# A token tower on one core: orders of five engines and homes of the banks by a plan of eleven steps with 27 added waits, in place of one of thirteen with 37

## The reference, cut to what matters

```python
h = take(table, x)                                   # embedding, f32
h = h + linear_attention(layernorm(h))               # L0_attn: elu features, cumulative sums in each row of 128 tokens
h = h + (layernorm(h) @ CB.T) * scale + bias         # L0_ffn
h = h + performer_block(layernorm(h))                # L1_attn: softmax features, projection, ff 256->1024->256, two norms
x = layernorm(h)                                     # L1_ffn
logits = x @ router_w.T                              # 8 experts, one is chosen for each token
xs = x * sigmoid(max(logits))
moe = (silu(xs @ gate[e]) * (xs @ up[e])) @ down[e]  # e = argmax(logits)
h = h + moe + silu(x @ shared_gate) * (x @ shared_up) @ shared_down
```

## Time and profile before

| | us |
|---|---|
| median of 3 runs | 658.73 (656.73 to 664.01) |
| the profiled execution | 657.52 |
| its span in the trace | 655.7 |
| PE busy | 617.5 |
| DVE busy | 466.2 |
| ACT busy | 317.8 |
| POOL busy | 278.4 |

### The profile page before, as it was taken

One profiled execution on the slowest core, in us unless ns is written; L12 is line 12 of the kernel. 1 busy time (PEld: TensorE's weight loads), 2 busy tenths in 40 slices (PEclk: granted clock), 3 DMA queues, 4 the chain that ended last, 5 costly groups with the idle time before them and its releaser, 6 DMA issues.

```text
span 655.7 us, 15603 instructions
## 1 busy us (share of the span) xinstructions
PE 617.5 (94%) x5960; PEld 503.3 (77%) x5960; DVE 466.2 (71%) x1108; ACT 317.8 (48%) x751; POOL 278.4 (42%) x534
## 2 busy tenths in 40 slices
PE   5987899999999999999999999999999698999997
PEld 4765688988888989898989889999999554554563
DVE  3697998999999988888889989768657432223322
ACT  3456576667566654756555556565332021212321
POOL 6263357345464353534333263352332334535433
PEclk9899999999999999999999999999999999999999
DMA  7960000000000000000000000000001259363551
GB/s 257 411 286 1 9 10 9 2 10 17 2 20 9 9 18 2 17 2 19 1 18 17 2 18 2 17 19 10 17 25 34 58 215 401 113 227 115 193 215 32
DMA packets 17369, 46.88 MB, mean 71 GB/s; under 512 B 6913, under 2 KB 11536, under 8 KB 14864
## 3 DMA queue, kind: packets, MB, share of 16 engines
q1 hardware_dynamic: 13136, 37.47, 15.2%
q0 software_dynamic: 4160, 8.41, 4.0%
HBM read 40.54 MB, written 6.89 MB: 72 GB/s over the span
## 4 chain that ended last, share of the span: by engine, by line
PE 77%; DVE 7%; DMA 6%; issue 3%; ACT 3%; POOL 2%; SPq 2%; POOLq 0%; DVEq 0%; ACTq 0%
PE ps L1150 71%; PE ps L1155 3%; DMA we<-w_experts 2%; PE ps L1311 2%; DMA home_rows<-send_home 1%; DMA x_rows<-send_x 1%; DVE stats L751 1%; SPq L318 1%; SPq L319 1%; DMA H_S<-table,idx_sb 1%; POOL rstd L422 1%; ACT qkA L729 1%; DVE rdenTA L826 1%; DVE H_S L803 0%; PE ps L1285 0%
## 5 line engine op out<-in xcount | busy, mean ns | idle before, releaser
L421 POOL TENSOR_TENSOR var_eps<-mv,ln_eps 128x1 f32<-128x1 f32 x112 | 24.2, 216 | 252.7 <-DVE mv L752 251.7
L1150 PE MATMUL ps<-yTC,we 128*128 128x128 f32 x1024 | 124.3, 275 | 0.0
L1150 PEld LDWEIGHTS ps<-yTC,we 128*128 128x128 f32 x1024 | 120.5, 192 | 1.0 <-issue 0.3
L1150 PE MATMUL ps<-we,yTA 128*128 128x256 f32 (+1 forms) x272 | 86.7, 449 | 4.3 <-issue 3.7
L422 POOL TENSOR_TENSOR rstd<-var_eps,pow_half 128x1 f32<-128x1 f32 x112 | 66.2, 591 | 8.8
L1150 PEld LDWEIGHTS ps<-we,yTA 128*128 128x128 f32 x272 | 49.7, 191 | 25.2 <-issue 21.1
L1150 PE MATMUL ps<-we,ffT 128*128 128x256 f32 x256 | 60.8, 380 | 0.0
L1150 PE MATMUL ps<-we,yTB 128*128 128x256 f32 (+1 forms) x176 | 52.9, 442 | 2.1 <-SPq L367 2.1
L1150 PEld LDWEIGHTS ps<-we,ffT 128*128 128x128 f32 x256 | 47.2, 190 | 5.6
L1150 PEld LDWEIGHTS ps<-we,yTB 128*128 128x128 f32 x176 | 32.0, 190 | 16.8 <-issue 13.9
L803 DVE TENSOR_TENSOR H_S<-ps,causal_sb 128x512 f32<-128x512 f32 x64 | 40.0, 668 | 2.2 <-PE ps L1150 2.2
(11 more groups left out here) (220 smaller groups left out, 1341.5 us busy)
## 6 DMA issues: line engine op xcount, KB each, us to landing
we<-w_experts SPq DMA_DIRECT2D x8, 1536.0 KB, 17.1
H_S<-w_experts SPq DMA_DIRECT2D x8, 1536.0 KB, 6.6
we<-w_ff SPq DMA_DIRECT2D x2, 1024.0 KB, 8.7
x_rows<-send_x SPq DMA_DIRECT2D x16, 128.0 KB, 1.7
home_rows<-send_home SPq DMA_DIRECT2D x16, 128.0 KB
rows_sb<-rows SPq DMA_DIRECT2D x1, 1664.0 KB
we<-w_qk SPq DMA_DIRECT2D x2, 512.0 KB
we<-w_v SPq DMA_DIRECT2D x2, 256.0 KB
```

The source lines that it names most:

```text
L421: link(pool.tensor_tensor(var_eps[:, k:k + 1], mv[:, k, 1:2], ln_eps[:], ALU.add))
L1150: return pe.matmul(o, a, b, start=start, stop=stop)
```

## The change

The steps, their operations, operands and numbers are the same. What changes is the order of each engine's list, the lags, the bank of each result, and the added waits (27). PE's lags reach 11, hence 27 turns; DVE's 11, ACT's 10, POOL's 10, SP's 8. The waits for operands stay. The banks of the experts' part are numbered afresh too.

```diff
-        dgT, T0, qk0, v0, nd0, o0 = (ps[:, 5, :], ps[:, 6, :], ps[:, 2, :], ps[:, 4, :], ps[:, 5, :], ps[:, 7, :])
+        dgT, T0, qk0, v0, nd0, o0 = (ps[:, 7, :], ps[:, 6, :], ps[:, 6, :], ps[:, 2, :], ps[:, 3, :], ps[:, 0, :])
...
             run_steps([
-                (4, home_out), (0, x_out), (9, ids2), (3, ids1), (9, ids3), (1, ids0),
+                (3, home_out), (1, ids0), (6, ids1), (8, ids2), (0, x_out), (8, ids3),
             ])
...
             def a_T0(t):
                 pe.wait_ge(S["src0_ready"], t + 1)
-                after(pe, "qexp_in", (t - 5) * 2 + 2)
-                after(pe, "scores_masked", (t - 2) * 4 + 1)
                 transposed(T0, yA).then_inc(S["src0T_psum"], 1)
...
             def a_v(t):
                 pe.wait_ge(S["src0T_ready"], t + 1)
-                after(pe, "ffb_ready", (t - 6) * 4 + 4)
-                after(pe, "v0_ready", t)
+                after(pe, "scores_masked", (t - 1) * 4 + 1)
...
             def b_kq(t):
...
                 if t + 3 < T:
                     after(pe, "scores_masked", (t + 3) * 4 + 3)
-                if t + 4 < T:
-                    after(pe, "x_ready", (t + 4) * 4 + 4)
+                after(pe, "tile_done", t - 6)
...
             def c_dn(t):
                 pe.wait_ge(S["hT_ready"], t + 1)
-                if t + 6 < T:
-                    after(pe, "out1_read", t + 7)
-                if t + 3 < T:
-                    after(pe, "logit_copied", t + 4)
+                if t + 9 < T:
+                    after(pe, "src1T_ready", t + 10)
...
             run_steps([
-                (6, b_out), (1, a_v), (11, c_ga), (0, a_T0), (5, b_kmB), (4, a_ffn), (7, c_f1), (12, c_dn),
...
+                (7, c_f1), (5, b_v), (5, b_kmB), (1, a_v), (4, a_ffn), (11, c_up), (9, c_cn), (7, c_f2), (8, c_T6),
+                (3, a_out), (10, c_ga), (8, c_lo), (6, c_T5), (2, a_num), (5, b_ctx), (2, a_den), (4, b_T3),
+                (5, b_qT), (5, b_cTT), (0, a_T0), (4, b_qk), (1, a_s), (11, c_dn), (0, a_qk), (5, b_h), (4, b_dg),
+                (4, b_kq), (4, b_dgT), (6, c_fa), (6, c_fb), (3, a_T2), (5, b_out), (4, b_kmT),
             ])
```

More of the change, by code:

```diff
@@ L709, in _ @@
             run_steps([
[L710 to L713, removed]
+                (10, c_th), (0, a_norm), (2, a_rd), (5, b_cT), (8, c_tt), (4, b_yT), (5, b_rqT), (1, a_par),
+                (0, a_yT), (5, b_cx2), (3, a_norm2), (4, b_x), (4, b_sq), (0, a_x), (8, c_send), (4, b_dgc),
+                (7, c_norm), (4, b_rk), (6, c_ra), (3, a_yT2), (0, a_exp), (6, c_rb), (4, b_ek), (4, b_keps),
+                (7, c_yT2), (4, b_eq), (3, b_norm), (5, c_yT),
             ])
@@ L1117, in _ @@
             run_steps([
[L1118 to L1122, removed]
+                (0, a_stats), (6, b_rec), (5, b_dgr), (6, b_mean), (5, b_km), (5, b_qs), (5, kmx), (6, b_o),
+                (5, b_ks), (6, b_x1), (4, a_ff), (5, b_vo), (9, c_slot), (1, a_max), (10, table2), (11, c_hid),
+                (9, table0), (7, c_o), (10, table3), (3, a_o), (8, c_log), (7, c_res), (1, a_elu), (10, c_gc),
+                (9, table1), (1, a_vz), (3, a_res), (2, a_rec), (5, b_cx), (2, a_mean), (1, a_m1), (1, a_m2),
+                (1, a_m3), (11, c_down), (8, c_choose), (1, a_m0),
             ])
@@ L1227, in a_out @@
                 pe.wait_ge(S["src1T_ready"], t + 1)
+                if t + 1 < T:
+                    after(pe, "scores_masked", (t + 1) * 4 + 3)
                 by_token(o0[:, 0:D], yTA1, out0_sb, KD).then_inc(S["out0_psum"], 1)
@@ L1238, in a_ffn @@
                 pe.wait_ge(S["src2T_ready"], t + 1)
+                if t + 2 < T:
+                    after(pe, "scores_masked", (t + 2) * 4 + 2)
                 by_token(ff0[:, 0:D], yTA2, cb_sb, KD).then_inc(S["ffn0_psum"], 1)
@@ L1242, in b_T3 @@
                 pe.wait_ge(S["src3_ready"], t + 1)
+                after(pe, "src5T_ready", t - 1)
                 transposed(T3, yB).then_inc(S["src3T_psum"], 1)
@@ L1358, in c_fa, with c_fb @@
                 pe.wait_ge(S["src5T_ready"], t + 1)
+                after(pe, "ff2_read", t)
+                by_channel(fa, yTC, ff1_sb, range(4)).then_inc(S["ffa_psum"], 1)
+            def c_fb(t):
+                if t == 0:
+                    pe.wait_ge(S["last_loaded"], 16 * 7)
+                pe.wait_ge(S["src5T_ready"], t + 1)
                 if t + 5 < T:
                     after(pe, "scores_masked", (t + 5) * 4 + 4)
-                by_channel(fa, yTC, ff1_sb, range(4)).then_inc(S["ffa_psum"], 1)
-            def c_fb(t):
-                pe.wait_ge(S["src5T_ready"], t + 1)
-                if t + 2 < T:
-                    after(pe, "diag_read", t + 3)
-                after(pe, "hT_ready", t - 4)
+                after(pe, "gC_ready", t - 3)
                 by_channel(fb, yTC, ff1_sb, range(4, 8)).then_inc(S["ffb_psum"], 1)
@@ L1432, in _ @@
             run_steps([
-                (6, b_out), (1, a_v), (11, c_ga), (0, a_T0), (5, b_kmB), (4, a_ffn), (7, c_f1), (12, c_dn),
-                (3, a_out), (9, c_cn), (5, b_qT), (7, c_f2), (2, a_num), (5, b_ctx), (2, a_den), (4, b_T3), (8, c_T6),
-                (6, c_T5), (5, b_cTT), (4, b_qk), (1, a_s), (0, a_qk), (11, c_up), (5, b_h), (4, b_dg), (4, b_kq),
-                (8, c_lo), (4, b_dgT), (6, c_fa), (3, a_T2), (6, c_fb), (4, b_kmT), (4, b_v),
+                (7, c_f1), (5, b_v), (5, b_kmB), (1, a_v), (4, a_ffn), (11, c_up), (9, c_cn), (7, c_f2), (8, c_T6),
+                (3, a_out), (10, c_ga), (8, c_lo), (6, c_T5), (2, a_num), (5, b_ctx), (2, a_den), (4, b_T3),
+                (5, b_qT), (5, b_cTT), (0, a_T0), (4, b_qk), (1, a_s), (11, c_dn), (0, a_qk), (5, b_h), (4, b_dg),
+                (4, b_kq), (4, b_dgT), (6, c_fa), (6, c_fb), (3, a_T2), (5, b_out), (4, b_kmT),
             ])
```

63 lines of the change are left out of this document (25 added, 38 removed).

## The result

660.93 us median (659.53 to 665.36, 20 runs) against 658.16 (654.28 to 664.71, 20 runs) of the kernel before: a ratio of 1.006, with a 95% interval of 1.0043 to 1.0077 (the two medians alone give 1.004). That is 0.6% slower, clear of no change but less than 1%. The profiled execution took 660.82 us, its span 659.0 us.

A forecast was written before the change was run, and what follows sets the result against it. PE's own work was taken as the bound in the middle. The terms 2.0 + 1.8 + 1.5 - 2.4 + 2.7 summed to +5.6 us, a span of 661.3 and an execution of 663.1 us, with a range of 655 to 670.

The forecast's parts named there:

- Added waits and banks, 0: Whole pipeline: ten fewer added waits and new banks change nothing, as met waits cost nothing visible; ends -1.5 and +1.5.
- no order can win more than those 3.1 us there: Middle of the kernel: PE's own work bounds it, with some 1.7 us lost per 100 us at most.
- The fill, +2.0: Start of the pipeline: `a_v` and `a_T0` behind `b_kmB` cost +2.6 over tiles 0 and 1, less 0.6 at `b_kq`.
- The two waits: Fill, as a sign: PE idle about 2 us right before `km_diag`'s matmul, twice, before 85 us.
- One more `c_up`, +1.8: Drain: one more `c_up` stands ahead of the last `c_cn` on PE and moves all behind it by 1.8 us.
- `c_down` ahead of `c_choose`, +1.5: Drain, DVE: the last `c_choose` stands behind `c_down`, which waits for a `home_rows` store slowed by a scatter; +1.5 us.
- SP's order, -2.4: Drain and late experts: one store less in the way, late weights load some 4 us sooner, ending waits; -2.4 us.
- The clock, +2.7: Start of the experts' part: PE mostly idles before the rows come, so its clock falls to 0.50; +2.7 us.
- the slower case: Each turn: ACT's steps between `a_den` and `a_s` stall PE, 0.5 us in 13 turns, +6.5; 668 to 672; chance 0.16.
- the faster rival: Fill and drain: a shorter pipeline pays, two tiles' waits (-4) and 3.2 us of drain idle go; -9, about 650; chance 0.10.

The follow-up runs named there:

- ten_waits: The changed kernel with ten more added waits on PE at `a_s`, all long met; 662.62 us, ratio 1.0088 to the kernel before.
- before_yt: The kernel before with one ACT step moved, `c_yT` ahead of `a_par`, `b_cx2` and `a_rd`; 654.79 us, ratio 0.9967 to the kernel before.
- place_up: The changed kernel with `c_down` adding into H (no store wait) and `c_up` behind `c_cn` on PE; 660.34 us, ratio 1.0045 to the kernel before.
- in_place: The changed kernel with `c_down` adding into the tile's rows of H, so without the store wait; 661.25 us, ratio 1.0058 to the kernel before.
- sp_old: The changed kernel with SP's list of the kernel before; 662.67 us, ratio 1.0073 to the kernel before.
- warm_gap: The changed kernel with 56 small matmuls behind PE's last pipeline step and 24 behind the experts' first transposes; 664.89 us, ratio 1.0088 to the kernel before.
- kmb_early: The kernel before with PE's `b_kmB` ahead of `a_v`, `c_ga` and `a_T0`; 667.40 us, ratio 1.0172 to the kernel before.

## Why the prediction was right, and where it was not

The time, 663 against 660.9, and the verdict (within 1%, on the slower side) were right, but partly by luck: errors in the sum have opposite signs. Between the two traces, in us of the span:

| part | predicted | measured |
|---|---|---|
| fill, up to `b_qk` of tile 2 | +2.0 | +3.3 |
| middle, from there to the last `c_f2` | 0 | -2.4 |
| the last `c_cn` (one more `c_up`, `c_down`) | +3.3 | +2.0 |
| from `c_cn` to the first product | 0 | +0.7 |
| first round (clock) | +2.7 | +2.2 |
| late weights | -2.4 | -2.2 |
| together (measured: with a rest of -0.3) | +5.6 | +3.3 |

- *Added waits and banks, 0.* That met waits cost nothing was right (`ten_waits`). The step that failed is the reading of the middle, "no order can win more than those 3.1 us there". It took busy time for work. A `b_qk` that takes 2.04 us is as busy as one of 1.95, and the turn fell by 0.46 us with PE busy as before. Of this 0.21 are ACT's late `c_yT`, shown by `before_yt`; 0.25 lie between or within other steps and are not settled. From `b_qk` of tile 7 to that of tile 12, five turns, it is 150.29 us before and 147.90 in the changed kernel, so 2.4 us came from the full turns. The two new idle times of the middle cost 0.37 + 1.17 us once; without them the middle would have won some 4 us (2.4 + 1.5), which is above the 3.1.
- *The fill, +2.0.* Measured +3.3. The two waits came as described. But in these traces their own cost is about 0.2 us; 3.1 are a fall of the clock that the prediction did not expect there: PE was busy 6.27 of the 10 us from 50 to 60, as before 6.21. The kernel before and `before_yt` have one order there, one without the fall and one with it, so the fall is not the order's alone. The 0.97 ahead of `b_kq` went, and `b_kq` started only 0.06 sooner.
- *One more `c_up`, +1.8.* It is there as work, but moving it back wins nothing (`place_up`): `c_choose` was not done sooner, and PE would have waited in its place. As a loss by the order it was not real.
- *`c_down` ahead of `c_choose`, +1.5.* The mechanism was right: the store took 8.24 us, and PE waited 2.17. `in_place` removes the wait in the trace; that the time falls with it no run shows. The route to the rows was seen less well: `c_slot` is behind `c_down` too.
- *SP's order, -2.4.* The wait went, and PE's last `c_dn` ended 14.2 us after `c_cn`, as said, with the loads at 26.8. But the list was not needed for it (`sp_old`).
- *The clock, +2.7.* Right: 5.90 us for 3.69, +2.2, at the place forecast, and in `warm_gap`, with the idle time filled, it is 3.69 again. All ten traces in which PE waited 1.1 us or more for the first rows, with nothing put into that time, have a slow first round (5.2 to 6.7 us); `before` and `before_yt`, without such a wait, do not. One trace speaks for a second cause: in `kmb_early` PE waited 0.25 us only, and the round took 5.09. The gain of `warm_gap` did not reach the time, though.

Of the rivals, no stall came between `a_den` and `a_s`, which was the slower case.

Two figures of the prediction do not follow from its rows, and the sum does not hang on either: PE's work behind the last `c_cn` is 14.77 us by the window and not 15.3, and the two terms of the faster rival, 4 and 3.2 us, make 7.2 and not 9.

The clock is more of the result than the profile of one execution tells. The mean granted clock of the 20 runs of the changed kernel was 0.981, that of 89 runs of the kernel before 0.987 (the profiled ones had 0.983 and 0.994). Among the 20, the twelve at 0.982 and above took 659.53 to 661.76 us, the eight below 662.35 to 665.36. Read as a slope, which is 0.47 us for each 0.001 both in these 20 and in the 89, 0.006 is some 3 us: about the whole difference between the two medians. That does not clear the orders, because the clock is no cause apart from them: one fall of 6.8 us takes 0.005 off the mean of 659 us. As an estimate, the changed kernel has about one such fall more than the kernel before has on average. It also means that the profiled execution of the kernel before flatters it: of the 89 only five had 0.994 or more.

No version here beats both kernels for certain. `before_yt` has the lowest median, 654.79 us, and its interval ends at 1.0001.

## What to carry to other kernels

Busy time is not work: where an engine is busy 99% of the time, take the pitch of one full turn, and of each step in it, before saying that no order can win. Many met waits are cheap, and one that is met late in every turn is not. A fall of TensorE's clock for 6.8 us cost 2 to 3 us here, more than a wait of 2 us ahead of it; it comes in some executions of the same instructions and not in others, so compare several traces before giving it to an order. Where a wait vanishes, look what it hid. A mean clock for each run belongs beside each time.

## What the hardware showed unexpectedly

- The clock fell at 56.0 us in the changed kernel, with no idle time of PE over 1.98 us in the 6 us ahead. In `before_yt` it fell at 55.2 behind the same instructions, and the same 7.06 of 10 us busy, at which it stayed up in the kernel before. Filled, it fell 24 us later, for 3.4 us and not 6.8.
- Ten waits for semaphores long met, on one step, left a full turn at 29.61 us.
- A store of 128 KB took 8.24 us beside a scatter of 128 numbers of 4 bytes, and 5.70 beside the last one.
